# A 32-tile transformer stack: set-up reordered, and five normalisations and every epsilon moved from VectorE to GpSimd

## What is computed

```
x = x + jnp.tanh(g_xattn[0]) * _L0_xattn_ref(ctx_2048, _layernorm(x, axis=-1), ...)   # 8-head cross attention
x = x + jnp.tanh(g_ffn[0]) * _L0_ffn_ref(_layernorm(x, axis=-1), ...)                 # 2 layers: rotary local attention + gated MLP
x = x + jnp.tanh(g_xattn[1]) * _L1_xattn_ref(_layernorm(x, axis=-1), ctx_2048, ...)   # RMS norm, linear, de-pooled patches
x = x + jnp.tanh(g_ffn[1]) * _L1_ffn_ref(_layernorm(x, axis=-1), ...)                 # top-2 of 8 low-rank experts
x = x + jnp.tanh(g_xattn[2]) * _L2_xattn_ref(ctx_2048, _layernorm(x, axis=-1), ...)   # 8-head attention on given keys
x = x + jnp.tanh(g_ffn[2]) * _L2_ffn_ref(_layernorm(x, axis=-1), ...)                 # ternary weights, 8-bit activations
x = x + jnp.tanh(g_xattn[3]) * _L3_xattn_ref(_layernorm(x, axis=-1), ctx_2048, ...)   # 16-head self + context attention
x = x + jnp.tanh(g_ffn[3]) * _L3_ffn_ref(_layernorm(x, axis=-1), ...)                 # ternary MLP with a depthwise conv
```

## Time and profile before

| | |
|---|---|
| median of 3 runs | 1537.61 us (1535.76 to 1540.38) |
| the profiled execution's own time | 1530.82 us |
| its span, first to last instruction | 1529.0 us |
| busy: PE, PEld, DVE, ACT, POOL | 1350.0, 936.1, 1355.9, 1041.2, 755.5 us |
| instructions: PE, DVE, ACT, POOL | 16078, 4086, 2053, 1147 |
| mean granted TensorE clock | 0.979 of full speed |

### The profile page before, as it was taken

The page is one execution under the profiler, slowest core; times in us unless marked ns, Lnnn a source line. Parts: engine busy times, 40 slices in busy tenths (PEclk is TensorE's granted clock), DMA queues, the critical chain, the costliest instruction groups (busy, mean ns, idle before and its releaser), DMA issues.

```text
span 1529.0 us, 42022 instructions
## 1 busy us (share of the span) xinstructions
PE 1350.0 (88%) x16078; PEld 936.1 (61%) x16078; DVE 1355.9 (89%) x4086; ACT 1041.2 (68%) x2053; POOL 755.5 (49%) x1147
## 2 busy tenths in 40 slices
PE   3888899998898899998998998998899998998977
PEld 2556666666566665666665665666666676665644
DVE  5888999889998999899998899999899888997876
ACT  1455768667676777677767767766776776776556
POOL 7766544555536644455445356256435545355110
PEclk9999999999999999999999999999999999999959
DMA  7002201111101211111101121111211111111110
GB/s 226 10 15 54 77 22 24 33 39 48 48 23 31 69 41 39 31 42 37 44 21 50 41 51 45 24 30 47 60 24 46 25 32 47 41 38 25 33 46 6
DMA packets 134071, 64.37 MB, mean 42 GB/s; under 512 B 98666, under 2 KB 124650, under 8 KB 133617
## 3 DMA queue, kind: packets, MB, share of 16 engines
q1 hardware_dynamic: 131281, 56.56, 14.6%
q10 hardware_dynamic: 2592, 5.12, 0.9%
HBM read 50.06 MB, written 2.14 MB: 34 GB/s over the span
## 4 chain that ended last, share of the span: by engine, by line
PE 41%; DVE 26%; ACT 16%; POOL 8%; issue 6%; POOLq 1%; DMA 1%; SPq 0%; ACTq 0%; DVEq 0%
PE ps_all L1447 6%; ACT L816 4%; PE ps_all L1732 3%; PE ps_all L1485 3%; DVE mx L1124 3%; PE ps_all L1511 3%; POOL wide_a L603 3%; POOL rden L603 3%; PE ps_all L1440 3%; PE ps_all L1524 3%; PE ps_all L1570 3%; DVE wide_b L1127 2%; DVE wide_b L1181 2%; PE ps_all L1688 2%; PE ps_all L1556 2%
## 5 line engine op out<-in xcount | busy, mean ns | idle before, releaser
L603 POOL TENSOR_TENSOR rstd<-rstd,minus_half 128x1 f32<-128x1 f32 x320 | 195.5, 619 | 513.3 <-DVE rstd L1102 512.5
L603 POOL TENSOR_TENSOR rden<-rden,minus_half 128x16 f32<-128x16 f32 x64 | 188.7, 2949 | 9.7 <-issue 0.5
L603 POOL TENSOR_TENSOR wide_a<-wide_a,wide_b 128x256 f32<-128x256 f32 x256 | 181.0, 739 | 2.2 <-DVE wide_b L1181 2.1
L854 ACT COPY wide_a<-ps_all 128x512 f32<-128x512 f32 (+1 forms) x192 | 139.4, 728 | 56.9 <-PE ps_all L1524 33.0
L1124 DVE TENSOR_REDUCE mx<-ps_all 128x8 f32<-128x512 f32 (+1 forms) x192 | 164.6, 859 | 14.6 <-PE ps_all L1538 5.0
L816 ACT ACT_TABLE_LOAD x131 | 168.1, 1283 | 2.3
L1447 PE MATMUL ps_all<-ident,wide_b 128*128 128x128 f32 x1024 | 153.0, 281 | 17.9 <-ACT wide_b L867 12.4
L1447 PEld LDWEIGHTS ps_all<-ident,wide_b 128*128 128x128 f32 x1024 | 115.9, 143 | 55.3 <-issue 22.2
L867 ACT ACTIVATE wide_b<-wide_b 128x512 f32<-128x512 f32 (+1 forms) x160 | 113.9, 715 | 38.5 <-DVE wide_b L1127 37.4
L1127 DVE TENSOR_TENSOR wide_b<-ps_all,mx 128x512 f32<-128x512 f32 (+1 forms) x160 | 126.7, 792 | 2.4
L1511 PE MATMUL ps_all<-w_qkv,ht_shift 128*128 128x512 f32 x256 | 123.7, 605 | 4.4 <-ACT ht_shift L877 2.9
(11 more groups left out here) (264 smaller groups left out, 3581.7 us busy)
## 6 DMA issues: line engine op xcount, KB each, us to landing
wide_c<-wide_c SPq DMA_DIRECT2D x128, 64.0 KB, 2.2
wide_a<-in_k SPq DMA_DIRECT2D x32, 256.0 KB, 2.6
wide_a<-in_k SPq DMA_DIRECT2D x64, 128.0 KB, 2.6
v_pad<-in_v SPq DMA_DIRECT2D x64, 128.0 KB, 2.8
v_pair<-in_v SPq DMA_DIRECT2D x32, 136.0 KB, 2.6
ctx_t<-in_ctx_t SPq DMA_DIRECT2D x32, 128.0 KB, 2.6
ctx_s<-in_ctx SPq DMA_DIRECT2D x32, 128.0 KB, 3.2
xin<-in_x SPq DMA_DIRECT2D x32, 64.0 KB, 2.6
```

Of the source, the lines that this page charges most:

```text
L603: return gp.tensor_tensor(o, a, b, op)
L854: a.copy(to, of).then_inc(*done(name))
```

## The change

Three edits, and new tables for them.

1. **Epsilon.** All ten `_eps` stages of a tile leave DVE. POOL adds the epsilon itself in front of the power, in the `_rstd` stage, with a drain between the two.
2. **Normalise.** The `_y` stage of `l0a`, `l0f`, `l1a`, `l2a` and `l3a` is now POOL's.
3. **Set-up.** POOL fills `rows` first and only the edges of the padded buffers; `v_pad` is filled in the first three tiles. ACT issues `raw` and `soon` at once, SP takes the weights `later`. Tiles 1 to 3 come in four joint loads. DVE sums `raw` before it waits for the bound's transpose.

```diff
     "dve": """   # per tile: l0a_eps l0a_y ... l3f_eps are gone, 10 _eps and 5 _y
     "pool": """  # per tile: l0a_y l0f_y l1a_y l2a_y l3a_y are new
@@ SP's set-up
+            load_now(now[:4])
             sp.wait_ge(signal("bias_split"), 1)
             ...
+            load_now(now[4:])
+            sp.wait_ge(signal("rows_zero"), 1)
             sp.wait_ge(signal("bias_kept"), 32)
-            sp.wait_ge(signal("consts"), 1)
             ...
+            load_more()
@@ POOL's set-up
+            gp.memset(rows[:], 0.0).then_inc(signal("rows_zero"), 1)
             gp.memset(tri[:], 1.0)
             ...
-            gp.memset(ht_shift[:], 0.0)
-            gp.memset(xt[:], 0.0)
-            gp.memset(v_pair[:], 1.0)
-            gp.memset(v_pad[:], 0.0)
+            gp.memset(ht_shift[:, :, :, 0:1], 0.0)
+            gp.memset(xt[:, :, :, 0:1], 0.0)
+            gp.memset(xt[:, :, :, ROW + 1:ROW + 2], 0.0)
+            gp.memset(v_pair[:, :, :, :, 16:17], 1.0)
@@ POOL's tile
-                def inv_std(n):
+                def inv_std(n, eps=LN_EPS):
 
                     yield f"{n}_rstd"
-                    tile(f"{n}_eps")
+                    tile(f"{n}_var")
+                    gp.tensor_scalar(rstd[:, s:s + 1], mv[:, s, 1:2], eps, None, ALU.add)
+                    gp.drain()
                     tt(rstd[:, s:s + 1], rstd[:, s:s + 1], minus_half[:, 0:1], ALU.pow).then_inc(*done(f"{n}_rstd"))
 
+                def normalise(n, of):
+
+                    yield f"{n}_y"
+                    tile(f"{n}_rstd")
+                    gp.tensor_scalar(y[:, s, :], of[:, s if of is x else i % EARLY, :], mv[:, s, 0:1], rstd[:, s:s + 1], ALU.subtract,
+                                     ALU.mult).then_inc(*done(f"{n}_y"))
@@ ACT's set-up
+            act.dma_start(raw, d["tern"]).then_inc(signal("tern_in"), 16)
+            for to, of in soon:
+                act.dma_start(to[:], of).then_inc(signal("weights_soon"), 16)
             act.wait_ge(signal("weights_now"), NOW)
@@ DVE's set-up
             v.tensor_reduce(bound[:], hit, AX.X, ALU.max).then_inc(signal("bound"), 1)
+            dve.wait_ge(signal("tern_in"), 16)
+            v.tensor_reduce(tern_sum[:], raw, AX.X, ALU.add, apply_absolute_value=True)
+            v.drain().then_inc(signal("tern_rows"), 1)
             dve.wait_ge(signal("bound_tp"), 1)
```

More of the change, by code:

```diff
@@ L80 @@
         l0a_dup l0f0_dup l0f1_dup second first third store
+        """.split(),
+    "load": """
+        later0 later1 later2
         """.split(),
@@ L99 @@
          "sp": ("sp", None)}
+ONCES = {"dve": "prep", "sp": "load"}
 ORDER = {
     "pe": """
[L102 to L105, removed]
@@ L194 @@
+        vpsqtvsrtsvuupvttvutvusrtvu
         """,
@@ L296, in in_turn @@
     if once:
-        stages["prep", 0] = once
+        stages[ONCES[engine], 0] = once
     for each in stages.values():
@@ L519, in load_plug, with load_more, load_now @@
                         signal(f"plug_in{e}"), 16)
+            def load_more():
+                e = slice(1, EARLY)
+                what = {
+                    "xin": (xin[:, e, :], d["x"][e].rearrange("i p d -> p i d")),
+                    "ctx_t": (ctx_t[:, e].rearrange("p i a k -> p i (a k)"),
+                              d["ctx_t"][e].rearrange("i p a k -> p i (a k)")),
+                    "mask_row": (mask_row[:, e, :], d["mask_f"][e].partition_broadcast(P)),
+                    "ctx_s": (ctx_s[:, e, :], d["ctx"][e].rearrange("i p d -> p i d")),
+                }
+                for name in FIRST_IN:
+                    to, of = what[name]
+                    sp.dma_start(to, of).then_inc(signal("first_more"), 16)
+            def load_now(which):
+                for to, of in which:
+                    sp.dma_start(to[:], of).then_inc(signal("weights_now"), 16)
             sp.dma_start(lens_i[:], d["lens_t"]).then_inc(signal("lens_in"), 16)
@@ L701, in _ @@
                 gp.drain()
-            for s in range(VALUES):
-                ends = v_pad[:, s].rearrange("p b (n m) w -> p (b n) (m w)", m=2)
-                gp.memset(ends[:, :, 8:57:48], 1.0)
             gp.drain().then_inc(signal("pads"), 1)
@@ L764, in chain @@
                 n.then_inc(*done("l0a_part"))
+                if i < VALUES:
+                    ends = v_pad[:, i].rearrange("p b (n m) w -> p (b n) (m w)", m=2)
+                    gp.memset(v_pad[:, i], 0.0)
+                    gp.drain()
+                    gp.memset(ends[:, :, 8:57:48], 1.0).then_inc(signal("value_pads"), 1)
                 yield from inv_std("l0f")
+                yield from normalise("l0f", x)
                 for L in range(2):
@@ L1096, in statistics @@
                     v.bn_aggr(mv[:, s, :], stats[:, s, 0, :]).then_inc(*done(f"{n}_var"))
-                def above_zero(n, eps=LN_EPS):
-                    yield f"{n}_eps"
-                    tile(f"{n}_var")
-                    ts(rstd[:, s:s + 1], mv[:, s, 1:2], eps, None, ALU.add).then_inc(*done(f"{n}_eps"))
-                def normalise(n, of=None):
-                    yield f"{n}_y"
-                    tile(f"{n}_rstd")
-                    ts(y[:, s, :], x[:, s, :] if of is None else of, mv[:, s, 0:1], rstd[:, s:s + 1], ALU.subtract,
-                       ALU.mult).then_inc(*done(f"{n}_y"))
                 def centre(n):
```

386 lines of the change are left out of this document (189 added, 197 removed).

## The result

The changed kernel takes **1578.3 us** (median of 4 runs, 1571.0 to 1582.4) against 1536.8 before (4 runs). The ratio is 1.0248, 95% interval 1.0212 to 1.0285, so 38 us slower. The forecast was 1510 us and its range ended at 1552. What was put down as the likeliest case didn't come; the rival "POOL becomes a wait on the path" did, in sign.

A forecast was written before the change was run, and what follows sets the result against it. It took PE and DVE, both 90.2% busy and in step, as the bound. Set-up -4.5, DVE's relief -24 and end +1.5 gave -27 us, from the median 1537.6 to 1510.6, said as 1510 us; range 1482 to 1552.

The forecast's parts named there:

- the likeliest case: Whole kernel: DVE's relief partly comes through, 1510 us, with its own range 1492 to 1530; chance 0.58.
- POOL becomes a wait on the path: Rival: `y` and power on POOL come up late behind rotary work; with 15 such waits 1555 us; chance 0.18.
- the one on latency: Normalisations: about 0.6 us later five times a tile, 0.2 us for the other five, hidden by eight tiles under way.
- The cover that wasn't one: POOL's queue: its 512.5 us of waits for DVE's epsilon were to cover 234 us of added work.
- The relief: Long stretch, 60 to 1470 us: DVE loses 67 us of work, giving 24 us of time; ends 0 and 67.
- The sizes: POOL and DVE instructions: `y` 0.80 us, addition with drain 0.33; busy time POOL about 990 us, DVE near 1284.
- The estimate of 0.69 us for `y`: `y` on POOL: alternative price from the skill's 1.8 cycles per element; the prediction kept 0.80 from the rows.
- The set-up's -4.5 us: Start of kernel: PE's first tile starts 2 to 6 us sooner, taken as 4.5, with DVE's set-up ending at 18.6.
- The end's +1.5: From 1470 us on: about three normalisations of the last tile's own chain, 0.5 us longer each.
- 30 waits of 2.9 us behind the rotary blocks: Inside the POOL rival: a quarter of 480 stages meet a rotary block, a quarter of these hurt; net +60 us.
- threshold of some 50 us: Test: the prediction is wrong if PE's or DVE's waits for POOL sum to more than this.
- an order planned for it can set the `y` early: Argument against the POOL rival: replanned fixed queues place `y` ahead of the rotary blocks; no size of its own.

The follow-up runs named there:

- kernel 6: Kernel before, with an idle addition and its drain on POOL in front of each power, epsilon still on DVE; ratio 1.0334, 51 us slower.
- kernel 5: Kernel before, with the same idle addition and drain on POOL behind each power, epsilon still on DVE; ratio 1.0108, 17 us slower.
- kernel 2: Kernel before, with the epsilons alone moved from DVE to POOL, otherwise old order and set-up; ratio 1.0206, 32 us slower.
- kernel 13: Kernel before, with an idle `y` and drain on POOL behind 160 powers, the real `y` kept on DVE; ratio 1.0293, 45 us slower.
- kernel 3: Kernel before, with the five `y` stages alone moved to POOL, each directly behind its power; ratio 1.0248, 38 us slower.
- kernel 1: Kernel before, with the new set-up alone, all stages and orders as before; ratio 1.0021, 3 us slower.
- kernel 4: Kernel before, with epsilons and five `y` both moved to POOL, old order and old set-up; ratio 1.0665, 102 us slower.
- kernel 11: Changed kernel with the old set-up put back; ratio to the kernel before 1.0217, 33 us slower.
- kernel 12: Kernel before, with only DVE's order edited so each epsilon stands directly behind its variance; ratio 1.0068, 10 us slower.

## Why the prediction was wrong

**The step that failed** is the one on latency: "With eight tiles under way in turn this is hidden as long as the other tiles' stages fill PE's queue". It let 0.6 us per full normalisation and 0.2 us per other one go at no cost. The sizes were near: from the variance's end, a `y` ended 0.54 us later in the changed kernel (86 us by 160) and the other five's powers 0.08 (12 by 160). That it is hidden was wrong: kernel 6 makes each power late by one addition and costs 51 us, of which 17 come without that lateness (kernel 5); kernel 2 costs 32. The condition was stated, but not checked, and the rows were there: PE already waited 8.7 us for `y` and DVE 10.6 us for the power, in orders that are fixed, so that at these places what comes later is waited for.

**The cover that wasn't one**, which failed as well: that POOL's "512.5 us of waits for DVE cover the 234 us" took a sum over the span for a sum at the places where work comes up. The row itself says otherwise: 182 waits, the longest 23.7 us, for 320 powers. The other 138 powers began without a wait of over 0.15 us, so they came up while POOL was busy. In the changed kernel POOL waited for the variance 131 times in 320 (88, 37 and 6 by its three lines). The work comes in clusters, and within one each added 0.38 or 0.81 us pushes what is behind it. Kernels 5 and 13 show this with nothing made late by its own added step: 17 us and 45 us.

**The relief.** That "a good third of DVE's goes away, 24 us" was a choice that nothing in the trace fixed, as the prediction says. It measured 7 us for 43.5 us less work on DVE (kernels 3 and 13; 0 to 14). For epsilon, 6 and 2 are 20 us apart, but 2's way is also shorter by 105 us in the sum, which at 0.21 to 0.29 us each would alone account for 22 to 30. That PE and DVE were equally busy at 90.2% didn't make them equal in worth: PE's waits for DVE stayed, 82 and 80 us.

**The sizes.** The prices of the instructions held: `y` 0.81 us for 0.80, the addition with drain 0.38 for 0.33, POOL 968 us for 990, DVE 1293.8 for 1284. The estimate of 0.69 us for `y`, worked out from the figure in the Trainium skill, GPSIMD Engine Reference, section Performance versus the Vector engine, did less well: the trace has 0.814, so here the nearest rows were the better guide. The set-up's -4.5 us measured +3, between -2 and +9 (kernel 1): in the changed kernel PE's first tile starts 0.83 us sooner, since DVE's set-up ends at 23.68 and `rows` is issued 3.1 us later than before, both against the forecast. The end's +1.5 can't be read off by itself.

**The rivals.** That POOL becomes a wait on the path was right as to the engine, and half right as to the mechanism. It counted 30 waits of 2.9 us behind the rotary blocks. What came were 53 waits of PE for `y` of 0.77 us in the mean. In 21 of them, 18.6 of the 40.6 us, POOL did rotary work between the variance's end and the `y`; in the other 32 it was its other short steps alone. DVE's waits for the power came on top. Its threshold of some 50 us for PE's and DVE's waits for POOL was passed (41 + 33). Against it I had set that "an order planned for it can set the `y` early". The order is worth 69 us (kernels 4 and 11), but not by this: the `y` end 558 us after their variances in kernel 4 and 556 in kernel 11, while the powers of the other five normalisations come 100 us sooner (392 and 292). What makes up the 69 us wasn't isolated. On the general rule: the Trainium skill, Perfetto Trace Analysis, section Optimizing GPSIMD Operations, advises preferring implementations on other engines where possible; the measured 814 ns beside 362 on DVE agrees, and so does the time.

**What stays open.** Why the five `y` cost 38 to 45 us at +88 to +90 us of lateness of the powers while the additions cost 0.21 to 0.29 per us isn't settled, and least of all for kernel 3, where the `y` themselves are hardly later. POOL's rotary work doesn't explain it: from the end of `den` to the end of the last rotary addition, 64 pairs, kernels 3, 13 and 5 all took 18 or 19 us more than before (447), at costs of 38, 45 and 17 us. That both moves together cost 32 us more than their sum was only seen, not taken apart. How much of the 11.4 us of longer PE work is the lower granted clock wasn't isolated.

## What to carry to other kernels

Idle time of an engine is room only where the work arrives. Before giving a half-idle engine more, count how many of its instructions start without a wait: those stand in a cluster, and each addition there delays the next (here 138 of 320, and 17 us lost by additions that nobody waited for). To price a move, put an idle copy of the moved instruction into the old kernel and leave the original in place: one such kernel gives the cost without the relief, and the difference to the real move bounds the relief, some 7 us of 43.5 here. It isn't the relief alone, since the original and the moved instruction also end at different times: sum both ways from the traces before reading it.

Moving work between engines in fixed orders has to be tried with the order replanned, which was worth 69 us, but a replanned order doesn't make a slower engine's longer way free.

## What the runs showed of the hardware

- The chain of waits shifts with the drains. The share of "issue" in it is 6 to 8% in the kernels without added drains, 16% in kernel 13 with 160 and 26 to 33% in those with 320. Kernel 5, 17 us slower, has POOL at 27% and "issue" at 26%; kernel 3, 38 us slower and without added drains, has POOL at 21% and "issue" at 8%. The chain's share of an engine doesn't rank the kernels.

```profile
POOL 27%; issue 26%; PE 16%; DVE 11%; POOLq 10%; ACT 7%; DMA 1%; SPq 1%; DVEq 0%; ACTq 0%
```

```profile
PE 34%; DVE 22%; POOL 21%; ACT 11%; issue 8%; POOLq 2%; DMA 1%; SPq 1%; DVEq 0%; another core or an unknown queue 0%; ACTq 0%
```

- On DVE, an epsilon that reads what the variance just ahead of it wrote starts 0.21 us behind that one's start (median of 320 in kernel 12). In the timeline of the kernel before, an epsilon directly behind its variance of line L1096 starts 0.21 us behind it (median of 84 places), the statistics of another tile in the same position 0.09 us (10 places).
- The mean granted clock fell from 0.979 to 0.962 while PE's idle time rose from 179 to 208 us. In the last stretch, where PE is busy 81% of the time, it was 0.76, as it was 0.79 before.
